# Three-valued weights used as such in the last layer, some remainders moved from VectorE to GpSimd, and smaller first loads

## What is computed

```
x = L0(x, ctx)      # attention to ctx, masked; + x; layer norm with gain and shift
x = L1(x, ctx)      # attention to ctx; + x; layer norm with gain and shift
x = x + SELF(ln(x)) # causal attention of x to itself
x = x + CROSS(ln(x), ctx)
x = x + relu(ln(x) @ w1 + b1) @ w2 + b2          # "FFN" below
x = x + L3(ln(x), ctx)                           # the last layer

def attention(xn, ctx):         # 16 heads of 16 columns
    q, k, v = xn @ Wq.T + bq, ctx @ Wk.T + bk, ctx @ Wv.T + bv
    p = softmax(q @ k.T / 4)    # per head
    return (p @ v) @ Wo.T + bo

# the last layer alone: each of its four weight matrices is first replaced by
def bit_quant(W):
    gamma = mean(abs(W))
    return clip(round(W / (gamma + 1e-5)), -1, 1) * gamma
```

## Time and profile before

| | us |
|---|---|
| median of 3 runs (1299.67, 1304.03, 1303.33) | 1303.33 |
| the profiled execution, its own time | 1301.78 |
| its span, first to last instruction | 1299.9 |
| TensorE (PE) busy | 1240.0, 95% |
| VectorE (DVE) busy | 1065.7, 82% |
| ScalarE (ACT) busy | 793.9, 61% |
| GpSimd (POOL) busy | 706.1, 54% |
| mean granted TensorE clock | 0.994 |

### The profile page before, as it was taken

One profiled execution on the slowest core, in us unless ns is written; L12 is line 12 of the kernel. 1 busy time (PEld: TensorE's weight loads), 2 busy tenths in 40 slices (PEclk: granted clock), 3 DMA queues, 4 the chain that ended last, 5 costly groups with the idle time before them and its releaser, 6 DMA issues.

```text
span 1299.9 us, 42570 instructions
## 1 busy us (share of the span) xinstructions
PE 1240.0 (95%) x18540; PEld 1016.2 (78%) x18540; DVE 1065.7 (82%) x1826; ACT 793.9 (61%) x1263; POOL 706.1 (54%) x847
## 2 busy tenths in 40 slices
...
GB/s 240 126 38 30 45 10 34 9 34 17 28 31 3 2 34 11 3 2 3 2 3 3 12 16 34 25 19 38 5 33 1 1 1 2 9 10 34 26 3 99
DMA packets 16594, 34.89 MB, mean 27 GB/s; under 512 B 2071, under 2 KB 7447, under 8 KB 15895
## 3 DMA queue, kind: packets, MB, share of 16 engines
...
## 4 chain that ended last, share of the span: by engine, by line
PE 55%; DVE 22%; POOL 10%; ACT 6%; issue 5%; DMA 2%; SPq 0%; POOLq 0%; DVEq 0%; ACTq 0%
DVE s_nm L1482 9%; PE ps L1111 7%; PE ps L996 6%; PE ps L1167 6%; PE ps L1179 5%; PE ps L1194 5%; PE ps L1148 5%; PE ps L1049 4%; PE ps L1008 3%; PE ps L1021 3%; ACT s_PU L1339 3%; DVE s_Os L1489 2%; DVE s_KH L1439 2%; PE ps L1126 2%; PE ps L1145 2%
## 5 line engine op out<-in xcount | busy, mean ns | idle before, releaser
L1482 DVE TENSOR_REDUCE s_nm<-ps 128x8 fp32r<-128x960 f32 (+1 forms) x352 | 398.1, 1160 | 40.2 <-PE ps L1049 19.0
L1339 ACT ACTIVATE s_PU<-ps 120x1024 f32<-120x1024 f32 (+1 forms) x288 | 281.9, 1023 | 110.6 <-PE ps L1126 109.6
L1667 POOL TENSOR_TENSOR s_Os<-s_Os,s_Rc 128x512 f32<-128x512 f32 x80 | 86.9, 1087 | 307.5 <-DVE s_Rc L1497 304.3
L1111 PE MATMUL ps<-s_Qs,s_KH 32*120 32x256 f32 (+2 forms) x4608 | 192.3, 289 | 13.3 <-DVE s_nm L1482 3.1
L1111 PEld LDWEIGHTS ps<-s_Qs,s_KH 32*120 32x120 f32 (+1 forms) x4608 | 154.6, 180 | 45.5 <-issue 13.0
L1167 PE MATMUL ps<-s_W,s_oT 128*128 128x256 f32 x960 | 134.5, 290 | 7.1 <-DVE s_oT L1411 6.2
L1148 PE MATMUL ps<-s_PU,s_Vp 120*32 120x256 f32 x2048 | 135.5, 388 | 4.2 <-DVE s_nm L1482 1.2
L996 PE MATMUL ps<-s_xT,s_W 128*128 128x256 f32 (+1 forms) x768 | 134.8, 324 | 3.3 <-DVE s_W L1416 1.0
L1167 PEld LDWEIGHTS ps<-s_W,s_oT 128*128 128x128 f32 x960 | 120.7, 191 | 16.4 <-issue 8.2
L1614 POOL TENSOR_TENSOR s_xs<-s_xs,s_rowv 128x512 f32<-128x512 f32 x96 | 125.2, 1304 | 11.4 <-POOL s_mv L1652 1.1
L1049 PE MATMUL ps<-s_KH,s_Qs 32*128 32x240 f32 x3072 | 126.9, 291 | 4.6 <-DVE s_nm L1482 2.4
...
## 6 DMA issues: line engine op xcount, KB each, us to landing
...
s_mi<-mask SPq DMA_DIRECT2D x8, 120.0 KB, 4.2
...
```

What stands on the lines that cost most here:

```text
L1111: t = e.matmul(banks[j][0:n, wide * x:wide * x + wide], kz[row[j], lk, g, c, k0:k0 + n], q[row[j], lq, g, qs_], start=(x == 0 and y_ == 0) ...
L1339: t = e.activation(P_of(i, k)[0:n, :, :], pair("B", i, k)[0:n, :, :], ACT.Exp, scale=0.25)
L1482: e.tensor_reduce(o, v, AX.X, ALU.max, negate=True).then_inc(sem["max"])
L1667: e.tensor_tensor(o[:, :, 0:16], o[:, :, 0:16], rc.to_broadcast([128, 32, 16]), ALU.mult).then_inc(sem["pool"])
```

## The change

- **Last layer's weights.** `TERNARY` names the last layer. `qw` now runs on VectorE in two operations and writes minus one, zero and one straight to the place of the weights (`s_W`); `Wh`, `Wl` and `wg` of this layer are gone. Such weights have no low part, so `parts_of` leaves out the third product: `K`, `V`, `O` have 8 matmuls instead of 12, a unit of `Q` 4 instead of 6. Gamma is multiplied in later, in operations that were there: `Th` and `Tl` (with the layer norm's gain, `gg`), `K0`, `Ve` and `y`.
- **Remainders of turned sums.** In the layers of `SPLIT` (first layer, CROSS, last layer) `OTl` is a GpSimd operation.
- **First loads.** The constants are loaded after the first weights, context and input, not ahead of them; the mask goes to 4 partitions instead of 128, with the rest set once by VectorE; `who` and `gone` are loaded later; `x` comes in eight loads of 512 KB instead of four of 1024 KB.
- **Order.** `WANT`, `AT` and the planner's costs are new, so every engine's order is new.

Core of the diff; of the two tables only one row is shown:

```
+TERNARY = ("L3",)
+SPLIT = ("L0", "CROSS", "L3", )
...
-    ("OTl", "L0"): (39.38, 52.07, 66.84, 80.42, 89.35, 101.27, 112.67, 131.41, 142.4, 154.37, 167.63, 180.57, 188.43, 204.07, 212.68, 226.02),
+    ("OTl", "L0"): (39.62, 52.48, 66.12, 77.92, 89.21, 103.35, 113.08, 130.16, 137.37, 151.15, 160.12, 172.5, 191.79, 201.76, 210.27, 221.95),
...
+def ready_of(layer, m):
+    return ("qw", m, 0) if layer in TERNARY else (rest_of(layer), layer, m)
+
+def parts_of(layer):
+    return PARTS[:2] if layer in TERNARY else PARTS
...
-            add("DVE", "OTl", after=[("OTh", i, 0)])
-            add("PE", "O", after=[("OTl", i, 0), (rest_of(layer), layer, 3)], rings=[("MI", ("O", i, 0), [("y", i, 0)])])
+            add("POOL" if layer in SPLIT else "DVE", "OTl", long=1.4 if layer in SPLIT else None, after=[("OTh", i, 0)])
+            add("PE", "O", long=.95 if layer == "L3" else None, after=[("OTl", i, 0), ready_of(layer, 3)], rings=[("MI", ("O", i, 0), [("y", i, 0)])])
...
-    for k in range(4):
+    p.add("SP", "msk", 0)
+    p.add("SP", "cst", 0)
+    for k in range(8):
...
-                p.add("POOL", "qw", m, after=[("qa", m, 0)])
-                last = ("qw", m, 0)
+                p.add("DVE", "qw", m, after=[("qa", m, 0)] + readers(*was))
+                if m == 0:
+                    p.add("PE", "wb", layer, m, after=[("qw", m, 0)], rings=[("MI", ("wb", layer, m), [("wa", layer, m)])])
+                    p.add("DVE", "wa", layer, m, after=[("wb", layer, m)])
+                continue
...
-                    for c, (cw, cx) in enumerate(PARTS):
+                    for c, (cw, cx) in enumerate(parts_of(layer)):
                         for k in range(2):
...
-                e.activation(xT_of(i)[:, 0, span_of(i, f), :], half_of("T", i, f), ACT.Copy).then_inc(sem["Th"])
+                    if layer_of(i) in TERNARY:
+                        w.wait_ge(sem["wa"], nth("wa", layer_of(i), 0))
+                        e.activation(to, half_of("T", i, f), ACT.Copy, scale=gg[:, f:f + 1]).then_inc(sem["Th"])
...
+            def qw(m):
+                over, under = (gq[:, 4 * m + k:4 * m + k + 1] for k in (2, 3))
+                to, low = (wv("L3", c, m).rearrange("p k n -> p (k n)") for c in range(2))
+                last = readers(*had_place("L3", m))
+                w.wait_ge(sem["qa"], 2 * nth("qa", m))
+                w.wait_ge(sem[last[0][0]], max(nth(*x) for x in last))
+                e.tensor_scalar(low, w3(m), under, None, ALU.is_lt).then_inc(sem["q1"])
+                w.wait_ge(sem["q1"], nth("qw", m))
+                e.scalar_tensor_tensor(to, w3(m), over, low.bitcast(f32), ALU.is_gt, ALU.subtract).then_inc(sem["qw"])
...
+            def OTlo(i):
+                o = oT[slot("oT", i)]
+                w.wait_ge(sem["OTh"], nth("OTh", i))
+                src = On[slot("On", i)][:, :, :].rearrange("p a n -> p (a n)")
+                behind()
+                e.tensor_tensor(o[:, 1, :, :].rearrange("p a n -> p (a n)"), src, o[:, 0, :, :].bitcast(f32).rearrange("p a n -> p (a n)"),
+                                ALU.subtract).then_inc(sem["pool"])
...
-            e.dma_start(cst[:, :], consts).then_inc(sem["d_cst"], 16)
...
-                e.dma_start(xs[:, 4 * n:4 * n + 4, :, :], x_nat[:, 4 * n:4 * n + 4, :, :]).then_inc(sem[f"d_x{n}"], 16)
+                e.dma_start(xs[:, 2 * n:2 * n + 2, :, :], x_nat[:, 2 * n:2 * n + 2, :, :]).then_inc(sem[f"d_x{n}"], 16)
...
-                e.dma_start(mi[slot("mi", i)][:, :], mask[i // 2].partition_broadcast(128)).then_inc(dma_ops["mi", i, 0][0], 16)
+                else:
+                    w.wait_ge(sem["cst"], 2)
+                e.dma_start(mi[slot("mi", i)][0:128:32, :], mask[i // 2].partition_broadcast(4)).then_inc(dma_ops["mi", i, 0][0], 16)
```

More of the change, by code:

```diff
@@ L349 @@
 ROWMASK = True
-TURN = .19
+TURN = {("whole", "rows"): .195, ("columns", "rows"): .3, ("rows", "whole"): .185, ("columns", "whole"): .2,
+        ("whole", "columns"): .03, ("rows", "columns"): .03}
 def layer_of(i): return LAYERS[i // B]
@@ L744, in make_plan @@
                 p.add("POOL", "Wl", layer, m, after=[("Wh", layer, m)])
-    p.add("DVE", "mc", 0, after=[("mci", 0, 0)])
+    p.add("DVE", "mc", 0, after=[("mci", 0, 0), ("cst", 0, 0)])
     for k in range(4):
         p.stages["exp", 0, k].after.append(("mc", 0, 0))
+    for i in range(2):
+        p.stages["Qh", i, 0].after.append(("cst", 0, 0))
+        p.stages["D", i, 0].after.append(("mc", 0, 0))
+    p.stages["K0", 0, 0].after.append(("cst", 0, 0))
+    for u in range(3):
+        p.stages["A", 2 * B, u].after.append(("msk", 0, 0))
     p.run()
@@ L884, in program @@
         for name, i, k in plan.order["POOL"]:
-            n_pool += len(both(i)) if name == "Xl" else {"bo": 1, "cap": 1, "rs": 4, "lng": 2, "Xl": 2, "Cl": 1, "Hl": 1, "nmul": 1, "Wl": 1, "qw": 3}[name]
+            n_pool += len(both(i)) if name == "Xl" else {"bo": 1, "cap": 1, "rs": 4, "lng": 2, "Xl": 2, "Cl": 1, "Hl": 1, "nmul": 1, "OTl": 1, "Wl": 1}[name]
             pool_ops[name, i, k] = n_pool
@@ L1018, in V @@
                 for j in range(2):
[L1019 removed]
+                    for c, (cw, cx) in enumerate(parts_of(layer)):
                         for k in range(2):
                             t = e.matmul(m[0:n, j * 256:j * 256 + 256], src[:, cx, k, n * j:n * j + n], wv(layer, cw, 2)[:, k, :],
[L1022 removed]
+                                         start=(c == 0 and k == 0), stop=(c == len(parts_of(layer)) - 1 and k == 1))
                 t.then_inc(sem["V"])
```

200 lines of the change are left out of this document (103 added, 97 removed), and 571 rows, old and new, of tables (AT, WANT).

## The result

The changed kernel takes **1284.3 us** (median of 4 runs, 1282.8 to 1285.1) against 1303.7 for the one before in the same session (4 runs, 1299.7 to 1307.6): ratio **0.985**, 95% interval 0.983 to 0.987. That is 19.3 us less; 25.8 were forecast. The profiled execution took 1283.6 us, 18.1 less than that of before.

The account below looks back on a forecast made before the run. TensorE, busy 95% of the span, was taken to bound the kernel everywhere. The terms 20.6 + 3.6 + 0.5 - 0.1 + 1.2 gave 25.8 us off, so 1277.5 us, range 1266 to 1291.

Parts of the forecast that it names:

- The last layer: Last layer: fewer matmuls take 24.0 us off TensorE, of which 2 us gained early and 18.6 behind, together 20.6 us.
- CROSS and tail: CROSS gains 0.5 us from a lighter VectorE; the last item's chain at the end gains 0.1 us.
- L1's share: Last layer from 1150 us: TensorE busy 95.2%, as in L1, so 121.4 us instead of 140.
- rival A: Last layer becomes a matter of waits, TensorE held at 89.8%: gain 11.3 us, 1292 us; chance 0.15.
- the ramp: Last layer's start, 1100 to 1150 us, TensorE busy 89.8%: 4 us of matmuls lie there, half counted, 2 us.
- `OTl` on GpSimd: First layer: a lighter VectorE gains 3.6 us, half of 7.3; the longer chain to `O` costs nothing, being hidden.
- Rival B: `OTl` on the path to `O`: 22 us added, only 20.6 and 1.2 gained, 1303.5 us; chance 0.04.
- New order elsewhere: L1, SELF and FFN: same work in another order, worth 0, bounds 2 us either way.
- First loads: Start of the kernel: earlier and smaller loads gain 1.2 us, bounds +4.3 and -0.5; first `K` near 6.2 us.
- last weights: Beside the FFN: sixteen GpSimd operations, some 21 us, and six on ScalarE gone, worth nothing.
- C: GpSimd's order makes `O` late, first layer above all: 43 us lost, kernel slower at 1325 us; chance 0.03.
- D: The order pays too: first layer and L1 reach 97.9%, gain 39.5 us in all, 1264 us; chance 0.10.

Follow-up runs that it names:

- The third product: The changed kernel with the third product made again in the last layer's Q, K, V and O: 1297.6 us, ratio 0.9955 to the kernel before.
- The waits of GpSimd: The changed kernel with GpSimd's `bo` and `Cl` of the last layer waiting for VectorE's nearby `Kl` pairs, all arithmetic kept: 1279.4 us, ratio 0.982.
- the old order: The changed kernel's code with the order tables of the kernel before, except first loads and the four `qw`: 1318.1 us, ratio 1.011.
- the kernel before with two products: The kernel before with only the third product left out in the last layer's Q, K, V and O: 1296.8 us, ratio 0.995.

## Why the prediction was right, and which step was off

The measured 1284.3 us lie within the stated range of 1266 to 1291 and 6.8 above the forecast of 1277.5. The gain came from the two sources named, TensorE's own matmuls and the first layer's idle time, but one step was wrong, and two terms agree by luck.

**The last layer (forecast 20.6 us, with CROSS and tail 21.0; the trace gives 15.6).** This term was too large. Its matmuls were well priced: 24.0 us by starts, 22.6 in the groups. The failing step is "I let TensorE have L1's share", 95.2%. Behind the layer's first `y` TensorE has 134.4 of 149.8 us, 89.8%, where the kernel before has 95.3%. The forecast's share left out the tail of 10 us; without it TensorE has 131.7 of 143.2 us, 92.0%, where the kernel before has 97.1%: at the mark of 92% that was set for rival A, and above its 89.8%. At 95.2% the same work would take 138.3 us, 4.9 less. That two engines nearly full can hold 95% in L1 did not carry over: in the last layer VectorE was also slowed, and some idle time came back as a lower clock. The third product shows how it adds up: 22.6 us of matmuls, less 4.9 of new idle time, less 3.9 of slower matmuls, makes 13.8. The prediction counted waits at their length only. It also put the gain in the wrong place: the third product is worth 5.0 us up to the layer's first `y`, where it gave the ramp 2, and 8.6 behind it, where it gave 18.6 together with the moved `OTl`.

I had named the collision, as what "strengthens rival A", and gave it no price. The waits of GpSimd price it: 4 to 5 us, nearly the 5.4 that this term lacks. Part of that was there before the change: the 16 `Kl` of the last layer take 867 ns each in the kernel before, 1068 in the changed one and 707 with the waits. The kernel before was not run with such waits, so how much of the 4 to 5 us is new stays open. The Trainium skill says it plainly (SBUF — State Buffer, Who interferes with whom): a VectorE instruction with two SBUF inputs contends with a GpSimd instruction that reads SBUF. This case's trace agrees, 0.7 us against 1.3 to 1.8. By that rule every `Kl` beside a long GpSimd operation should have been priced at up to 1 us more, some 6 us in the last layer, before VectorE's 109 us were set beside TensorE's 115.6. The price could be read from the trace of before: three pairs of `Kl` there take 2.16, 2.30 and 2.05 us in the last layer, the others 1.34.

**`OTl` on GpSimd (forecast 3.6 in the first layer; 3.4).** Right in size, but by luck of the reference point. The move is worth 11 us there in the new order, since with it VectorE would have held the first layer at 206.2 us, and about 15 us to the bad, over the whole kernel, in the old one. That I "cost this at nothing, because other items' work hides it" holds only since the order had been made for it. Rival B's 22 us, with 4% of the chance, is nearly what the old order pays: 20.5 us of waits for `OTl`.

The Trainium skill (Perfetto Trace Analysis, Optimizing Scalar/DVE Operations) says that offloading from a saturated VectorE may make sense, and that between VectorE and GpSimd it might not help because of the shared port. Both halves are seen here: -11 us in the first layer, +3 us in the last.

**New order elsewhere (forecast 0, bounds 2).** L1 and SELF lost 3.2 us, over the bound of 2, L1's 2.6 by itself. "The same work in another order" was true of the instructions and not of what stands beside them: in L1 a pair of `Kl` met four `lng`, and 2.17 us of PE's waiting came of it. How much of the other 2 us of idle time are such meetings stays open.

**First loads (1.2; 1.6) and last weights (0).** The first `K` starts at 5.96 us, 0.67 earlier, for 0.43 forecast. But TensorE's idle time up to the first `y` did not fall, though that was the forecast (10.5 before, 10.7 after); its busy time did, by 1.8 us, with the granted clock at 1.00 instead of 0.97. And the kernel before with two products, which has the old loads, reached its first `y` at 47.9 us as well, at a clock of 1.00. So beyond the earlier `K` no run shows what the loads are worth, and the agreement of 1.6 with 1.2 is luck. FFN showed no loss from the last weights; neither was tried alone.

**Rivals.** A's mechanism, waits for VectorE, was at work in the last layer; its time was too long because it gave nothing to the other parts and took too low a share. C didn't come, but its mechanism did in the old order, at 1318 us. D did not come. Of the signs set beforehand, PE's busy time, 48 `OTl` at 1.3 us, under 10 us of waits for them and the first `K` came true. The share of 95% behind the ramp did not, and the time from CROSS to the last `y` fell by 15.6 us and not 21.
